# Causal attention on one core: scores from 32 rows of the array, products for the maxima in pairs, q rotated on GpSimd

## What is computed

```python
q = proj(Wq, bq); k = proj(Wk, bk); v = proj(Wv, bv)     # 16 heads of 8 features
q = rope(q); k = rope(k)                                 # real parts alone: 4 features of 8 stay
scores = q @ k.T / sqrt(8)
scores = where(causal, scores, -1e10)
y = softmax(scores) @ v                                  # 4 batches x 16 heads x 1024 x 1024
out = x + (y @ Wo.T + bo)
```

## Time and profile before

| | before |
|---|---|
| time, median of three runs (lowest, highest) | 1768.23 us (1767.26, 1769.22) |
| the profiled execution: time, span of its instructions | 1769.27 us, 1767.2 us |
| TensorE busy, its mean granted clock (1 is 2.4 GHz, 0.5 is 1.2 GHz) | 1212.8 us (69% of the span), 0.814 |
| VectorE busy | 1021.9 us (58%) |
| ScalarE busy | 629.5 us (36%) |
| GpSimd busy | 510.0 us (29%) |
| reductions for the maxima (L1829, VectorE) | 768, 405.2 us |
| exponentials (L1603, ScalarE) | 384, 300.3 us |
| score products (L1719 and L1731, TensorE) | 235.1 and 201.1 us |

### The profile page before, as it was taken

One profiled execution on the slowest core, in us unless ns is written; L12 is line 12 of the kernel. 1 busy time (PEld: TensorE's weight loads), 2 busy tenths in 40 slices (PEclk: granted clock), 3 DMA queues, 4 the chain that ended last, 5 costly groups with the idle time before them and its releaser, 6 DMA issues. The chain is left out here.

```text
span 1767.2 us, 26688 instructions
## 1 busy us (share of the span) xinstructions
PE 1212.8 (69%) x9140; PEld 801.2 (45%) x9214; DVE 1021.9 (58%) x2340; ACT 629.5 (36%) x989; POOL 510.0 (29%) x571
## 2 busy tenths in 40 slices
PE   4625977959635059704888998899889997412991
PEld 2413856839524059702343443344434443311991
DVE  5855555655426136446777776777777770630662
ACT  4632221222111023201265664665566665001330
POOL 2434013040026747712003000300120000374772
PEclk9666988969755579955699998999999998555995
DMA  1439611020120133160000010001000100213325
GB/s 45 155 145 390 266 37 59 0 95 0 36 63 28 53 106 99 52 185 6 7 19 7 10 46 8 7 7 43 8 7 8 31 7 13 62 53 90 98 68 162
DMA packets 109057, 114.06 MB, mean 65 GB/s; under 512 B 8720, under 2 KB 90512, under 8 KB 108048
## 3 DMA queue, kind: packets, MB, share of 16 engines
q1 hardware_dynamic: 96608, 91.98, 16.5%
q0 software_dynamic: 9216, 19.02, 3.2%
q10 hardware_dynamic: 3120, 1.57, 0.3%
HBM read 49.34 MB, written 59.02 MB: 61 GB/s over the span
## 5 line engine op out<-in xcount | busy, mean ns | idle before, releaser
L1829 DVE TENSOR_REDUCE att_mx<-att_ps 128x1 f32<-128x512 f32 (+3 forms) x768 | 405.2, 555 | 146.9 <-PE att_ps L1722 111.3
L1603 ACT ACTIVATE att_prob<-att_ps 128x1024 f32<-128x1024 f32 (+3 forms) x384 | 300.3, 812 | 228.9 <-PE att_ps L1734 176.7
L1719 PE MATMUL att_ps<-att_kT,att_q1T 128*128 128x512 bf16 (+3 forms) x709 | 235.1, 344 | 50.5 <-DVE att_mx L1829 34.2
L1731 PE MATMUL att_ps<-att_q2T,att_kT 128*128 128x512 bf16 (+3 forms) x753 | 201.1, 331 | 3.2 <-ACT att_prob L1603 1.2
L1719 PEld LDWEIGHTS att_ps<-att_kT,att_q1T 128*128 128x128 bf16 x768 | 74.2, 98 | 259.1 <-DVE att_mx L1829 211.7
L978 POOL DMA_INDIRECT sides<-moe_ys,moe_back_i x160 | 153.2, 958 | 87.6 <-issue 47.3
L1745 PE MATMUL att_pso<-att_prob,att_v 128*32 128x512 f32 (+3 forms) x1536 | 163.9, 499 | 1.6
L972 POOL DMA_INDIRECT slots<-moe_rows,moe_place_i x128 | 123.2, 963 | 59.4 <-issue 38.4
L1499 POOL CAST att_qm_rows<-att_nm 128x32 bf16<-128x32 f32 x48 | 15.6, 324 | 395.8 <-DVE att_nm L1838 391.6
L1722 PE MATMUL att_ps<-att_mask,att_identb 128*128 128x128 bf16 x512 | 115.8, 228 | 2.3 <-DVE att_mx L1829 1.5
L1071 PE MATMUL moe_ps_t<-moe_ident,moe_xs 128*128 128x128 f32 x160 | 27.0, 290 | 115.2 <-DMA moe_xs<-slots 115.2
(11 more groups left out here) (283 smaller groups left out, 2439.5 us busy)
## 6 DMA issues: line engine op xcount, KB each, us to landing
slots<-fw_zeros SPq DMA_DIRECT2D x2, 5200.0 KB, 30.1
moe_xs<-slots SPq DMA_DIRECT2D x16, 650.0 KB, 4.9
sides<-fw_zeros SPq DMA_DIRECT2D x2, 4096.0 KB, 35.3
moe_side<-sides SPq DMA_DIRECT2D x16, 512.0 KB, 6.2
tok<-prep_tok SPq DMA_DIRECT2D x4, 1536.0 KB, 5.4
turned<-prep_tT SPq DMA_DIRECT2D x4, 1536.0 KB, 8.7
fw_tok<-tok SPq DMA_DIRECT2D x4, 1536.0 KB, 10.4
fw_Tkv<-turned SPq DMA_DIRECT2D x4, 1024.0 KB, 6.7
```

The source lines that it names most:

```text
L1603: nc.scalar.activation(prob[(2 * n + pair) % 4][:, :, 0:size], ps2[pair][:, :, 0:size], ACT.Exp, scale=SCORE_SCALE).then_inc(exp_done, 1)
L1719: last = nc.tensor.matmul(out[:, 0:size], q1T[t % 2][:, j * P:(j + 1) * P], kT[t][h][:, 512 * c:512 * c + size], start=True, stop=not diag ...
L1731: last = nc.tensor.matmul(ps2[pair][:, h, 0:size], kT[t][2 * pair + h][:, i * P:(i + 1) * P], q2T[t % 2][:, first:first + size], start=Tru ...
L1829: nc.vector.reduce_max(mx[:, c, j, h:h + 1], ps1[(n * QUAD + h) % 2][:, 0:size], AX.X).then_inc(max_done, 1)
```

## The change

Six things change, all within the attention stage.

1. `kT` is one tile per quad, as transposed, and `kT_all`, `place_keys`, its semaphore and the memsets are gone. Score products take both operands' 32 rows of one head. The masks still take 128 rows.
2. TensorE issues the maxima of a step two heads at a time, heads 2 and 3 before the first pair of exponentials and heads 0 and 1 before the second. VectorE reduces in that order of heads.
3. In a pair of exponentials both score products come first, then both masks.
4. q's rotation and split move from VectorE to GpSimd, where k's follow them (the first batch's stay on VectorE).
5. Normalising x moves from VectorE to GpSimd, in all four batches; the statistics move from step 1 to step 0.
6. The services of the preparation move one step earlier, and a step's middle service comes before the second pair of maxima.

```diff
-        kT = [[sb(f"kT{s}{h}", [P, SEQ], BF16) for h in range(QUAD)] for s in range(HEADS // QUAD)]
-        kT_all = sb("kT_all", [P, SEQ], BF16)
+        kT = [sb(f"kT{s}", [P, SEQ], BF16) for s in range(HEADS // QUAD)]
...
+        TURNS = (2, 3, 0, 1)
+
+        def head_rows(h):
+            return slice(32 * h, 32 * h + 32)
...
-        PREP = {(4, "mid"): "x0", (5, "mid"): "x1", (7, "mid"): "qk0", (8, "mid"): "qk1", (9, "mid"): "qk2", (10, "mid"): "qk3"}
+        PREP = {(3, "mid"): "x0", (4, "mid"): "x1", (6, "mid"): "qk0", (7, "mid"): "qk1", (8, "mid"): "qk2", (9, "mid"): "qk3"}
...
-            def place_keys(count, t):
-
-                wait(sp, misc_free, 1 + count + 1)
-                for h in range(QUAD):
-                    rows = slice(32 * h, 32 * h + 32)
-                    sp.dma_start(kT[t][h][rows, :], kT_all[rows, :]).then_inc(k_placed, 16)
...
-                nc.gpsimd.tensor_tensor(rstd[:], vareps[:], negh[:], ALU.pow).then_inc(rstd_done, 1)
+                nc.gpsimd.tensor_tensor(rstd[:], vareps[:], negh[:], ALU.pow)
+                pool.drain()
+                for j in range(TILES):
+                    last = nc.gpsimd.tensor_scalar(xn[:, j], xb[:, j], mv[:, j, 0:1], rstd[:, j:j + 1], ALU.subtract, ALU.mult)
+                last.then_inc(xn_done, 1)
...
                 if S.prep:
                     wait(pool, misc_free, 1 + S.count("qk3") + 1)
-                    rotate(nc.gpsimd, 1)
-                    for n in range(3):
-                        last = split(nc.gpsimd, 1, n)
-                    last.then_inc(k_split, 1)
+                    for k, done in ((0, q_split), (1, k_split)):
+                        rotate(nc.gpsimd, k)
+                        for n in range(3):
+                            last = split(nc.gpsimd, k, n)
+                        last.then_inc(done, 1)
...
                 if use == "k":
-                    keys_from_misc(count, G + 2)
+                    from_misc(count, kT[(t + 2) % QUADS][:], psm_b)
...
-            def max_step(G, t, n, heads=range(QUAD)):
+            def max_step(G, t, n, turns=range(QUAD)):
...
-                for h in heads:
-                    u = G * (STEPS * QUAD) + (n * QUAD + h)
-                    out = ps1[(n * QUAD + h) % 2]
+                for i in turns:
+                    u = G * (STEPS * QUAD) + (n * QUAD + i)
+                    out = ps1[(n * QUAD + i) % 2]
+                    rows = head_rows(TURNS[i])
                     diagonal = P * (j + 1) == 512 * c + size
                     pe.wait_ge(max_done, u + 1)
-                    last = nc.tensor.matmul(out[:, 0:size], q1T[t % 2][:, j * P:(j + 1) * P], kT[t][h][:, 512 * c:512 * c + size],
+                    last = nc.tensor.matmul(out[:, 0:size], q1T[t % 2][rows, j * P:(j + 1) * P], kT[t][rows, 512 * c:512 * c + size],
                                             start=True, stop=not diagonal)
...
                 for h in range(2):
-                    last = nc.tensor.matmul(ps2[pair][:, h, 0:size], kT[t][2 * pair + h][:, i * P:(i + 1) * P], q2T[t % 2][:, first:first + size],
+                    rows = head_rows(2 * pair + h)
+                    last = nc.tensor.matmul(ps2[pair][:, h, 0:size], kT[t][rows, i * P:(i + 1) * P], q2T[t % 2][rows, first:first + size],
                                             start=True, stop=(i < 4 * c))
-                    if i >= 4 * c:
+                if i >= 4 * c:
+                    for h in range(2):
                         last = nc.tensor.matmul(ps2[pair][:, h, 0:P], identb[:], mask[:, 1], start=False, stop=True)
...
                     if quad:
-                        max_step(*quad, [0])
+                        max_step(*quad, [0, 1])
                     exp_step(S.G, S.t, n, 0)
-                    if quad:
-                        max_step(*quad, [1])
-                    exp_step(S.G, S.t, n, 1)
-                    if quad:
-                        max_step(*quad, [2])
                     if (n, "mid") in S.uses:
                         serve(S, S.uses[n, "mid"])
+                    if quad:
+                        max_step(*quad, [2, 3])
+                    exp_step(S.G, S.t, n, 1)
...
-                    if quad:
-                        max_step(*quad, [3])
                     if (n, "end") in S.uses:
...
-                    if S.prep and n == 1:
+                    if S.prep and n == 0:
                         statistics(S.b + 1)
-                    if S.prep and n == 3:
-                        normalize(S.b + 1)
-                    if S.prep and n == 10:
-                        dve.drain()
-                        rotate(nc.vector, 0)
-                    if S.prep and n == 11:
-                        split(nc.vector, 0, 0)
-                    if S.t == 2 and S.more2 and n < 2:
-                        last = split(nc.vector, 0, n + 1)
-                        if n == 1:
-                            last.then_inc(q_split, 1)
```

More of the change, by code:

```diff
@@ L1823, in _, with maxima @@
         def _(dve):
-            def maxima(G, t, n, heads=range(QUAD)):
+            def maxima(G, t, n, turns=range(QUAD)):
                 j, c = MAX_STEPS[n]
                 size = min(512, P * (j + 1) - 512 * c)
-                for h in heads:
-                    dve.wait_ge(s1_done, G * (STEPS * QUAD) + (n * QUAD + h + 1))
-                    nc.vector.reduce_max(mx[:, c, j, h:h + 1], ps1[(n * QUAD + h) % 2][:, 0:size], AX.X).then_inc(max_done, 1)
+                for i in turns:
+                    h = TURNS[i]
+                    dve.wait_ge(s1_done, G * (STEPS * QUAD) + (n * QUAD + i + 1))
+                    nc.vector.reduce_max(mx[:, c, j, h:h + 1], ps1[(n * QUAD + i) % 2][:, 0:size], AX.X).then_inc(max_done, 1)
             def negate_maxima(G, first=False):
@@ L1848, in statistics @@
                 last.then_inc(stats_done, 1)
-            def normalize(batch):
-                dve.wait_ge(rstd_done, batch + 1)
-                for j in range(TILES):
-                    last = nc.vector.tensor_scalar(xn[:, j], xb[:, j], mv[:, j, 0:1], rstd[:, j:j + 1], ALU.subtract, ALU.mult)
-                last.then_inc(xn_done, 1)
             def consume(use, count, t, batch):
@@ L1924, in _ @@
             dve.wait_ge(weights_in, 7 * 16)
[L1925 removed]
+            for use in FIRST_USES[0:first_count("v0")]:
                 consume(use, first_count(use), 0, 0)
[L1927 to L1929 removed]
             dve.drain()
```

29 lines of the change are left out of this document (4 added, 25 removed).

## The result

The changed kernel took 2067.86 us (median of 4 runs, 2045.89 to 2079.86) against 1768.72 us for the kernel before (4 runs): the ratio is 1.1646, with a 95% interval of 1.1554 to 1.1738; it compares mean times and leaves out the longest of the four runs, 2079.86 us, as a slow one. The forecast was 1815 us with a range of 1738 to 1895. The sign was right, the size was not: +299 us instead of +47.

The account below looks back on a forecast made before the run. TensorE's queue was taken to bound the attention stage, VectorE's hand-back of two PSUM banks second. Terms 67 + 1 + 3 - 29 + 3 + 2 = +47 us gave 1816, or 1815 against the median; range 1738 to 1895.

Parts of the forecast that it names:

- rival B: Attention slots: 32-row products and form-change gaps halve the clock for a third of the stage, +130 us; chance 0.12.
- GpSimd's relief and its costs: Attention stage: VectorE's removed work, -29 us over three batches, with GpSimd's late keys, +3 us.
- Form changes: Plain slot on TensorE: 92 more changes between 32-row, full and value products at 0.09 us, +8.3 us.
- Rival A: TensorE in the slots: a change of rows costs nothing, total 1740 us; chance 0.18.
- the 0.16 of a drain: TensorE form changes: if each waits for the matmul in flight, 0.16 us apiece, 14.7 us a slot, about 1905 total.
- Overlap: Plain slot on TensorE: score products on different row groups stream together, -6.2 us.
- rival C: Score pairs on TensorE do not stream together: 6.2 us in 14 slots, +87, total 1903 us; chance 0.08.
- Order: Plain slot: maxima issued two at a time make TensorE wait for banks, +2.7 us, between 0 and 5.6.
- VectorE relieved: Around preparing slots: VectorE's removed work cuts waits for reductions by 9.8 us, three times, -29 us.
- GpSimd's late keys: Slot after a preparation: GpSimd's rotation and split end 1 us late each time, +3 us, between 0 and 6.
- Start: Before the first slot: key placing -1.8, memsets -2.2, GpSimd normalising +1, form changes in maxima +5; +2 us.
- What would show it: Signs in the slots: load 0.15 us after a mask, pair starts under 0.01 apart, plain slot 41 us, clock near 0.99.

Follow-up runs that it names:

- one_row_group: Changed kernel with masks on 32 rows too and every head's products on rows 0 to 31, so none overlap; 2212.47 us.
- relief: Kernel before with normalising and q's rotation and split on GpSimd, services one step earlier; 1839.88 us, ratio 0.9988.
- full_rows: Changed kernel with scores on 128 rows again, on zero-padded keys placed by DMA; 1900.74 us, ratio 1.0311.
- exp_32: full_rows with only the exponentials' score products cut to a head's 32 rows, masks full; 1892.56 us, ratio 1.0341.
- max_32: full_rows with only the maxima's score products cut to a head's 32 rows, masks full; 1988.52 us, ratio 1.0865.
- rows_only: Kernel before with 32-row scores and no key placing, old order and VectorE's work kept; 2198.99 us, ratio 1.2031.

## Why the prediction was wrong, step by step

**The step that failed** is the one that left the clock at 0.99 and gave its fall a chance of 0.12 (rival B). The argument was that the mean of 0.99 over 615 us "has every stall of the stage in it". That is true and does not bear on the change: the stalls were of TensorE between full products, and the change altered the products. I read the low clock before the first slot as the cost of waiting; *one_row_group* shows a low clock with TensorE busy for 97% of the time. B had half of the mechanism, the 32-row products, and named the gaps beside them, which the experiments clear; and it had them for a third of the stage, by its +130 a third of the slots. The fifteen slots at 0.67 mean two thirds of the time, and by the 66 us above the work of 8.6 slots.

B's price of a slot was near: 41.3 + 24.8 + 4 = 70 us at half clock, where the two plain slots above give 66. That is 22 more than at full clock and not 29; 4 of the 7 between are the form changes, which hardly grew. It was the share that was too small. By difference the clock cost 157 to 193 us: the measured 862.2, less the 648.2 of the new order with full rows, less 15 times 1.4 to 3.8 for the 32-row forms, 21 to 57. This takes every slot to cost what the plain one did. The other way comes to the same: 0.67 over 862.2 us is 569 us at half clock, which at 44 for 66 would have taken 190 less; and 44 lies in the 42.3 to 44.7 that 40.9 and 1.4 to 3.8 make. The waits for reductions hardly moved with the clock: 10.9 us in the plain slot of 63.0 us, 9.6 in that of 51.0.

Where 270 us went, over the fifteen slots:

| part | forecast of its steps | measured | from |
|---|---|---|---|
| GpSimd's relief and its costs | -26 | -9 | *relief*, 582.9 - 592.3 |
| order of the pairs | 2.7 a slot | 4.4 a slot, +65 | *full_rows* - *relief* |
| form changes less overlap | 2.1 a slot | 1.4 to 3.8 a slot, +21 to +57 | plain slots of *exp_32*, *max_32* |
| clock | 0 | +157 to +193 | the rest |

**Form changes.** 0.09 us from the value products was right for a change of rows: 0.10, and 0.11 at low clock. Rival A, that it costs nothing, is out, and so is the 0.16 of a drain, the estimate that the prediction worked out from the Trainium skill's page TensorEngine Tiling (Array Packing), Key Properties. The count of 92 was right too (116 less 24). But the step took all of them as path. Some 40% fell into time in which TensorE would have waited for a bank: 5.4 us for 87 of them, at 0.10 each 8.7.

**Overlap.** Pairs start 0.003 us apart, so rival C is out. What the saving is worth, *exp_32* shows only together with its changes: with 3.8 us saved and 44 changes of 0.10 paid in full it should have cost +0.6 us in a plain slot, and it cost +0.2; with 60% of the changes, 2.6, the overlap came to 2.4. The sum of changes and overlap, forecast at 8.3 - 6.2 = +2.1, lies in the 1.4 to 3.8 measured, but that owes something to luck: the changes came to 60% of 92 x 0.10, 5.5, and so the overlap must have come to 1.7 to 4.1 us rather than 6.2. Two errors cancelled. Stream time that is saved between two reductions would then come back as a wait for the next bank, just as a change is hidden in one. This is an inference from the sums; no kernel had the overlap alone.

**Order.** Right in kind: TensorE comes back to a bank before the reduction is done. In the plain slot, waits for reductions rose from 10.3 and 0.4 us to 11.0 and 2.8 (the waits of *full_rows* above), 3.1 together. What the step left out is that the services now stand between two pairs and wait too, for the copies that free their buffer: 0.9, 0.8 and 0.8 us in that slot, of which only 0.4 was there before. 4.4 measured, within the bounds of 0 and 5.6, not 2.7.

**VectorE relieved.** Forecast -29, with another 3 us given back for the keys; measured -9 in the slots, -5 in the stage. The step shared the extra waits out by the work removed. Only the part in the slot after came true, 6 us each time. In the preparing slot TensorE then waited for what the moved work delivers, normalised rows and projections, and not for banks: the extra waits for reductions went from 14.3 us to none, more than the 9.8 of the step, and the batch gained 3.8 at the first preparation. A wait that went was not time that went. The removed cover was real and the next thing was late: the question asked of GpSimd ("fits, at no cost") should have been asked with its own duration. Its normalising was put at 3 us, from the output bias row; it took 6.25. Eight operations of 128 elements don't cost what one of 1024 does.

**GpSimd's late keys.** Put at 1 us each, measured 0.3: right that they barely matter; the 17 us from start to end are close to the 19 forecast.

**Start.** Put at +2; the first q2T copy comes 5.1 us later. From the start of the stage to the first maximum it is 52.7 us, not 51.0: +1.7 where -1.8 - 2.2 + 1 = -3 was forecast. Normalising on GpSimd costs 4.3 there (*relief*), not 1, and the keys' part gives 2.5, not 4.0: *rows_only*, which has it alone, takes 42.8 us from the first statistics to the first maximum, where before took 45.3. The maxima before the first slot then take 3.7 more, forecast +5.

**What would show it.** The loads behind the mask (907.59 after 907.43, 0.16) and the pair's starts came out as written. The plain slot of 41 us did not come out, it took 51 to 63; that *full_rows* takes 40.9 is chance, since it has the order's cost alone and neither changes nor overlap. The sign of the clock's share was named there, and it decided.

## What to carry to other kernels

A product of a few rows saves no stream time by itself, and on this chip a stage made of them runs partly at half clock however gapless it is. Before cutting rows, ask what fills the other rows at the same moment; zero-padding to 128 rows was 214 us cheaper here. Price a change in the form of the products with the clock as a term of its own, since a mean clock measured with other products says nothing about it. And when work moves to a slower engine, take the moved operation's own duration there, then look at who reads its result, before counting the waits that go.

## What the hardware showed that I had not expected

- Granted clock of the fifteen slots: 0.53 with products of 32 rows on one row group and TensorE busy 97% of the time, 0.75 with pairs of them on different groups and 32-row masks, 0.96 with only the exponentials' products on 32 rows, 0.99 with 128 rows. How the chip weighs rows, columns and overlap is open.
- A change between 128 and 32 rows took 0.10 us at 2.4 GHz and 0.11 at 1.2 GHz, one from 128 to 32 columns 0.10 and 0.14, while a stream of 512 columns took 0.21 and 0.42.
- GpSimd's tensor_scalar on 128 x 128 float32 took 0.78 us, VectorE's 0.26.
- At the loop's end TensorE stands still for some 3 us in both kernels, with nothing to wait for that the profile shows. The timeline of before has it at 1066.88 to 1070.35:

```profile
1066.66 0.22 PE L1722 MATMUL att_ps<-att_mask,att_identb 128*128 128x128 bf16 x1
1070.35 0.61 PE L1719 MATMUL att_ps<-att_kT,att_q1T 128*128 128x512 bf16 x1 [3.47 <-issue]
```

The preparing slot that holds it took 51.3 us at a granted clock of 0.90. That of the last batch stands still as well, for 2.95 us at 1234.73, and took 47.4 at a clock of 1.00; the first, entered without the loop's jump back, took 44.4 at 1.00. So the standstill itself costs 3 us, and the other 4 came with the low clock.
